# Small products put between large ones on TensorE's turns outside its loop, a narrower wait of VectorE, and a residual product moved at the end

## The reference, cut to what matters

```python
xn = layernorm(x) * ln_w + ln_b
q = softmax(xn @ Wq + bq, over the 32 of a head)
k = softmax(xn @ Wk + bk + (1 - mask) * -1e6, over the 64 tokens)
v = (xn @ Wv + bv) * mask
att = einsum('bnhd,bnhl->bhdl', k, v)
y   = einsum('bnhd,bhdl->bnhl', q, att)
scale, shift = split(silu(emb) @ W_emb + b_emb)
hh  = silu((layernorm(y) * ln2_w + ln2_b) * (1 + scale) + shift) @ W_out + b_out
out = x + hh
```

## Time and profile before

| | us |
|---|---|
| median of 3 runs | 306.57 |
| lowest and highest of them | 304.46 and 307.16 |
| the profiled execution | 304.73 |
| its span, first instruction to last | 302.9 |
| PE busy in the span | 291.5 (96%) |
| DVE busy | 267.8 (88%) |
| POOL busy | 244.5 (81%) |
| ACT busy | 237.2 (78%) |
| granted clock of PE, mean | 0.999 |

### The profile page before, as it was taken

How to read it: one execution, slowest core, us unless ns; L and a number is a source line. 1 busy time by engine, 2 the same in 40 slices (tenths; PEclk the granted TensorE clock), 3 DMA queues, 4 the chain that set the end, 5 groups by cost and what they waited for, 6 DMA issues and landing times.

```text
span 302.9 us, 14378 instructions
## 1 busy us (share of the span) xinstructions
PE 291.5 (96%) x5530; PEld 248.2 (82%) x5530; DVE 267.8 (88%) x637; ACT 237.2 (78%) x592; POOL 244.5 (81%) x248
## 2 busy tenths in 40 slices
PE   7999899999999999999999999999999999999985
PEld 6578787989889898889888898989888898877764
DVE  4898999989999999999999999999999796977773
ACT  1555779697989889888989798888989798786543
POOL 2376489898998989998999989898999979873560
PEclk9999999999999999999999999999999999999999
DMA  6962560806335170907245270806151331002024
GB/s 207 307 244 67 162 188 5 245 4 186 134 115 200 43 269 1 303 9 227 85 133 179 74 239 1 312 1 249 63 183 60 101 142 50 21 4 72 4 71 138
DMA packets 28445, 38.61 MB, mean 127 GB/s; under 512 B 2433, under 2 KB 20481, under 8 KB 28418
## 3 DMA queue, kind: packets, MB, share of 16 engines
q1 hardware_dynamic: 28000, 37.94, 38.1%
q10 hardware_dynamic: 418, 0.30, 0.4%
HBM read 29.80 MB, written 8.45 MB: 126 GB/s over the span
## 4 chain that ended last, share of the span: by engine, by line
PE 86%; DVE 4%; POOL 4%; issue 2%; DMA 1%; ACT 1%; SPq 0%; DVEq 0%; POOLq 0%
PE bk L1156 29%; PE bv L1156 28%; PE by L1156 15%; PE by L1241 4%; PE by L1218 4%; PE bv L1230 4%; DMA x_all<-in_x 1%; DVE xstat L818 1%; POOL x_all L479 1%; POOL xr L459 1%; ACT k_t L661 1%; POOL k_t L428 1%; POOL xr L488 1%; DVE w_qv_lo L893 0%; PE by L1382 0%
## 5 line engine op out<-in xcount | busy, mean ns | idle before, releaser
L661 ACT ACTIVATE k_t<-k_t,kmax 128x64 f32<-128x64 f32 x240 | 60.5, 337 | 5.8 <-DVE kmax L952 5.6
L479 POOL TENSOR_TENSOR x_all<-x_all,bo_all 128x1024 f32 (+1 forms) x16 | 40.1, 2508 | 0.2
L448 POOL TENSOR_TENSOR xt_raw<-xt_raw,rows 128x512 f32<-128x512 f32 x28 | 36.3, 1298 | 4.2 <-DMA rows<-rows_dram 4.2
L450 POOL TENSOR_TENSOR xt_raw<-xt_raw,rows 128x512 f32<-128x512 f32 x28 | 36.1, 1290 | 2.2
L439 POOL TENSOR_TENSOR h_lo<-h_s,h_hi 128x512 fp32r<-128x512 f32 x28 | 35.4, 1287 | 0.5 <-ACT h_hi L680 0.4
L289 POOL TENSOR_TENSOR z_s<-z_s,mod_shift 128x512 f32<-128x512 f32 x30 | 30.7, 1046 | 5.4 <-DVE z_s L966 5.2
L615 ACT ACTIVATE y_s<-y_s,yr 128x256 f32<-128x256 f32 x56 | 29.1, 592 | 5.3 <-POOL yr L471 5.3
L1156 PE MATMUL bv<-w_o_hi,h_hi 128*128 128x256 f32 x112 | 29.4, 284 | 0.0
L1156 PE MATMUL bv<-w_o_lo,h_hi 128*128 128x256 f32 x112 | 28.9, 280 | 0.0
L600 ACT ACTIVATE v_s<-bk,small 128x256 f32<-128x256 f32 x32 | 15.2, 475 | 17.3 <-PE bk L1156 16.0
L1156 PEld LDWEIGHTS by<-kv,q_t 32*64 32x64 f32 x2048 | 22.4, 130 | 7.8 <-issue 5.8
(11 more groups left out here) (171 smaller groups left out, 863.7 us busy)
## 6 DMA issues: line engine op xcount, KB each, us to landing
x_all<-in_x SPq DMA_DIRECT2D x15, 512.0 KB, 6.4
out<-x_all SPq DMA_DIRECT2D x15, 512.0 KB, 5.1
xt_raw<-in_x_t SPq DMA_DIRECT2D x14, 512.0 KB, 5.9
rows<-rows_dram SPq DMA_DIRECT2D x14, 512.0 KB, 4.2
off<-in_mask_rows SPq DMA_DIRECT2D x16, 256.0 KB, 6.0
rows_dram<-xr_rows SPq DMA_DIRECT2D x56, 1.0 KB
x_all<-in_x SPq DMA_DIRECT2D x2, 256.0 KB, 3.7
z_s<-in_w_emb SPq DMA_DIRECT2D x1, 512.0 KB, 7.0
```

What stands on the lines that cost most here:

```text
L448: nc.gpsimd.tensor_tensor(xc, xc, rows[:, parity, 0, :], ALU.mult).then_inc(xm_d, 1)
L450: nc.gpsimd.tensor_tensor(xc, xc, rows[:, parity, 1, :], ALU.add).then_inc(xs_d, 1)
L479: nc.gpsimd.tensor_tensor(xg, xg, bo_all[:, :].unsqueeze(1).broadcast_to([P, T, D]), ALU.add).then_inc(xb_d, 1)
L661: last = nc.scalar.activation(kk, kk, ACT.Exp, scale=-1.0, bias=kmax[:, c, n:n + 1])
```

## The change

- `x_variances` waits for `xmv_d` (the `bn_aggr` of the group before) in place of `xr_d`; the wait for `xr_d` stands ahead of `x_means` now.
- `qv_tile`, `attention` and `y_product` are cut into parts: `qv_part(i, t, n)` is two matmuls of a tile, `attention_tile` and `y_tile` are the products of one tile (16 in the code, 32 pairs in the trace). In turns 2 and 15 PE issues them in turn: attention tile 0, then three times two q/v matmuls of tile 0 and an attention tile, then q/v tile 1; later y tiles 0 and 1, two q/v matmuls of tile 2, y tiles 2 and 3, and the rest of q/v tile 2. The loop's turns and turn 1 keep the order of before.
- In the tail, `x_added(M, 0, bv_)` and the wait for `res_d` ahead of it stand before `half_y_transposed(0)` instead of behind the two tile products.
- `late_out(e)` makes all products with the high part of both tiles, waits for the low part, and makes those with the low part.

```diff
@@ x_variances, x_means (DVE)
-                wait(dve, xr_d, 4 * g)
+                wait(dve, xmv_d, 4 * g)
...
             def x_means(g):
 
+                wait(dve, xr_d, 4 * g)
                 for t in range(T):
@@ qv_tile (PE)
+                for n in range(3):
+                    qv_part(i, t, n)
+
+            def qv_part(i, t, n):
+
+                if n > 0:
+                    pass
+                elif t < 2:
                     wait(pe, qsub_d, 4 * i + t - 3)
                     wait(pe, zs_d, 2 * (i - 2) + t + 1)
                 else:
                     wait(pe, kadd_d, 2 * i + t - 1)
                 tok = slice(t * P, t * P + P)
...
+                a = xt_lo if n == 2 else xt_hi
+                w = w_qv_lo if n == 1 else w_qv_hi
+                for c in range(C):
+                    last = mm(bqv[t][:, :], a[:, c, tok], w[:, c, :], n + c == 0, n == 2 and c == C - 1)
+                if n == 2:
+                    last.then_inc(qv_d, 1)
@@ body (PE)
+                apart = isinstance(i, int) and i >= 2
...
+                if B and apart:
+                    attention_tile(i - 1, 1 - par, 0)
+                    for n in range(3):
+                        qv_part(i, 0, n)
+                        attention_tile(i - 1, 1 - par, n + 1)
+                else:
+                    if B:
+                        attention(i - 1, 1 - par)
                     qv_tile(i, 0)
-                    qv_tile(i, 1)
+                qv_tile(i, 1)
                 if B:
                     wait(pe, h_d, 2 * i - 2)
-                    y_product(i - 1)
-                if F:
+                if B and apart:
+                    y_tile(i - 1, 0)
+                    y_tile(i - 1, 1)
+                    qv_part(i, 2, 0)
+                    y_tile(i - 1, 2)
+                    y_tile(i - 1, 3)
+                    qv_part(i, 2, 1)
+                    qv_part(i, 2, 2)
+                else:
+                    if B:
+                        y_product(i - 1)
                     qv_tile(i, 2)
-                    qv_tile(i, 3)
+                qv_tile(i, 3)
@@ late_out (PE)
-                if e == 0:
-                    pe.wait_ge(hhi_d, 2 * M + 2)
-                out_tiles(bv_[e], h_hi_m, h_lo_m, e,
-                          (lambda: pe.wait_ge(hlo_d, 2 * M + 2)) if e == 0 else None, False).then_inc(o_d, 1)
+                pe.wait_ge(hhi_d, 2 * M + 2)
+                for t in (2 * e, 2 * e + 1):
+                    dst = bv_[e][:, (t % 2) * D:(t % 2) * D + D]
+                    for c in range(C):
+                        mm(dst, h_hi_m[:, c, t * P:t * P + P], w_o_hi[:, c, :], False, False)
+                        mm(dst, h_hi_m[:, c, t * P:t * P + P], w_o_lo[:, c, :], False, False)
+                pe.wait_ge(hlo_d, 2 * M + 2)
+                for t in (2 * e, 2 * e + 1):
...
+                last.then_inc(o_d, 1)
@@ tail (PE)
                 x_added(L, 0, bk_)
+                pe.wait_ge(res_d, 2 * (L - 2) + 2)
+                x_added(M, 0, bv_)
                 half_y_transposed(0)
                 pe.wait_ge(zs_d, 2 * M + 2)
                 x_added_tile(2, bk_[1])
                 x_added_tile(3, bt[0])
-                pe.wait_ge(res_d, 2 * (L - 2) + 2)
-                x_added(M, 0, bv_)
                 x_added(M, 1, bv_)
```

More of the change, by code:

```diff
@@ L1195, in qv_tile @@
             def qv_tile(i, t):
-                if t < 2:
+                for n in range(3):
[4 more added lines that the diff above has]
+                elif t < 2:
                     wait(pe, qsub_d, 4 * i + t - 3)
@@ L1245, in attention @@
             def attention(g, parity):
-                wait(pe, ek_d, 2 * g + 2)
-                wait_apart(pe, v_d, 4 * g + 4)
                 for t in range(T):
-                    for c in range(C):
-                        col = (t * C + c) * AW
-                        for h in range(HC):
[L1252 to L1271, removed]
+                    attention_tile(g, parity, t)
@@ new lines, in attention_tile @@
+            def attention_tile(g, parity, t):
+                if t == 0:
+                    wait(pe, ek_d, 2 * g + 2)
+                    wait_apart(pe, v_d, 4 * g + 4)
+                for c in range(C):
+                    col = (t * C + c) * AW
+                    for h in range(HC):
+                        ch = c * P + h * DH
+                        for e in range(2):
+                            rows = slice(e * SEQ, e * SEQ + SEQ)
+                            last = mm(be[e][h * DH:h * DH + DH, col:col + AW], e_k[rows, t, ch:ch + DH],
+                                      v_s[rows, parity, t, c * HC + h, :], True, True)
+                if t == T - 1:
+                    last.then_inc(att_d, 1)
@@ new lines, in y_product, with y_tile @@
+            def y_product(g):
+                for t in range(T):
+                    y_tile(g, t)
+            def y_tile(g, t):
+                if t == 0:
+                    wait(pe, kv_d, 2 * g + 2)
+                    wait(pe, qt_d, 2 * g + 2)
+                for c in range(C):
+                    col = (t * C + c) * AW
+                    for e in range(2):
+                        b = 2 * t + e
+                        for h in range(HC):
+                            rows = slice(h * DH, h * DH + DH)
+                            last = mm(by[e * SEQ:e * SEQ + SEQ, h, col:col + AW],
+                                      q_t[rows, c, b * SEQ:b * SEQ + SEQ], kv[rows, b, c, :], True, True)
+                if t == T - 1:
+                    last.then_inc(y_d, 1)
@@ L1299, in late_out @@
             def late_out(e):
-                if e == 0:
-                    pe.wait_ge(hhi_d, 2 * M + 2)
-                out_tiles(bv_[e], h_hi_m, h_lo_m, e,
-                          (lambda: pe.wait_ge(hlo_d, 2 * M + 2)) if e == 0 else None, False).then_inc(o_d, 1)
+                pe.wait_ge(hhi_d, 2 * M + 2)
+                for t in (2 * e, 2 * e + 1):
+                    dst = bv_[e][:, (t % 2) * D:(t % 2) * D + D]
+                    for c in range(C):
+                        mm(dst, h_hi_m[:, c, t * P:t * P + P], w_o_hi[:, c, :], False, False)
+                        mm(dst, h_hi_m[:, c, t * P:t * P + P], w_o_lo[:, c, :], False, False)
+                pe.wait_ge(hlo_d, 2 * M + 2)
+                for t in (2 * e, 2 * e + 1):
+                    dst = bv_[e][:, (t % 2) * D:(t % 2) * D + D]
+                    for c in range(C):
+                        last = mm(dst, h_lo_m[:, c, t * P:t * P + P], w_o_hi[:, c, :], False,
+                                  t == 2 * e + 1 and c == C - 1)
+                last.then_inc(o_d, 1)
             def x_transposed(g):
@@ L1352, in body @@
                     q_transposed(i - 1, 1 - par)
-                    attention(i - 1, 1 - par)
-                if F:
-                    if isinstance(i, int) and i == 0:
-                        pe.wait_ge(weights_ready, 2)
+                if first(i):
+                    pe.wait_ge(weights_ready, 2)
+                if B and apart:
[6 more added lines that the diff above has]
+                        attention(i - 1, 1 - par)
                     qv_tile(i, 0)
-                    qv_tile(i, 1)
+                qv_tile(i, 1)
                 if B:
                     wait(pe, h_d, 2 * i - 2)
-                    y_product(i - 1)
-                if F:
+                if B and apart:
[9 more added lines that the diff above has]
+                        y_product(i - 1)
                     qv_tile(i, 2)
-                    qv_tile(i, 3)
+                qv_tile(i, 3)
                 if second(i):
```

## The result

| | before | after |
|---|---|---|
| median of 22 runs each, same chip, us | 305.03 | 306.69 |
| the profiled execution, us | 304.73 | 306.54 |
| its span, us | 302.9 | 304.8 |

The ratio after to before is 1.0044 (95% interval 1.0027 to 1.006): slower by 1.3 us, clear of zero and still within 1%. The forecast was 1.05 us faster. Its 305.5 us lies near 306.69 only by luck: the three runs of before that it was built on had a median 1.5 us above that of the 22. The sign is wrong, and the gain and the loss have to be told apart.

What follows compares the result with a forecast made beforehand. PE, busy 96% of the span, was taken as the bound. Terms: turn 2 +0.5, turn 15 -0.2, statistics' wait -0.9, end -0.45, together -1.05 us, from 306.57 to 305.5 us; range 303.4 to 307.3.

Steps and rivals of the forecast that it cites:

- Interleaving, attention: Turns 2 and 15: attention with q/v tile 0 takes about 2.65 us (bounds 2.2 and 3.1), so `att_d` comes later.
- Interleaving, y: Turns 2 and 15: `y_d` 1.6 us after y's start; turn 2 costs 0.5 us, turn 15 gives 0.2 back.
- speed from the store: Small products on PE: the first ones after large products run faster, taken as 0.5 us off attention with q/v tile 0.
- The wait: Before y of turns 2 and 15: PE idles 0.7 to 0.9 us for DVE's h products, 2.4 us behind `att_d`.
- PE would be even: Turn 2: q/v tile 3 ends at 55.7 us, 55.81 before, if the hole is covered, so PE loses nothing.
- the cases: Whole kernel: the forecast and its three rivals, from 303.6 us (holes all gained) to 307.3 us (late att_d).
- the late att_d costs more than the rest gains: Rival, turns 2 and 15: they cost over 1.35 us together; +0.75 us, 307.3 us; chance 0.15.
- The order does nothing: Rival, turns 2 and 15: instruction blocks come later as PE does, holes reappear further on; -0.15 us, 306.4 us; chance 0.25.
- The h products don't hold y back: Rival, turns 2 and 15: DVE's chain catches up, all three holes are gained; -3.0 us, 303.6 us; chance 0.15.
- Statistics' wait: Turn 0, DVE: its 1.12 us wait for POOL's scale goes, y of turn 1 starts earlier; 0.9 us gained (bounds 0 and 1.1).
- no new bound: Rows' transfer for turn 2: it starts 1.1 us earlier from DVE and limits nothing.
- The end: Tail: `x_added(M, 0)` fills PE's idle 1.46 us, second half transposes start at 292.13 for 292.60; gain 0.45 us (0 to 0.86).

Runs made afterwards that it cites:

- s10: s2 with 4 in place of 9 warming products at the start, ten load-and-matmul pairs fewer: 305.68 us, ratio 0.9998 to the kernel before.
- s2: The changed kernel with TensorE's order as before, leaving the statistics' wait and the end's edits: 303.69 us, ratio 0.9951 to the kernel before.
- s11: s2 with, in turn 15 only, two q/v matmuls put ahead of attention's last tile: 302.63 us, ratio 0.9899 to the kernel before.
- s3: The kernel before with only the changed statistics' wait: 303.97 us, ratio 0.9955.
- s4: The kernel before with only the end's edits, `late_out` and the moved `x_added(M, 0, bv_)`: 305.40 us, ratio 1.0004.
- s1: The kernel before with only the new order of TensorE in turns 2 and 15, attention and y: 308.87 us, ratio 1.0117.
- s5: The kernel before with only attention interleaved with q/v tile 0 in turns 2 and 15, y in one piece: 308.02 us, ratio 1.0084.

## Why the prediction was wrong, point by point

**The step that failed is the size of the interleaved products: 2.65 us for attention with q/v tile 0 in "Interleaving, attention", and 1.6 us from y's start to `y_d` in "Interleaving, y".** They measured 3.28, above the upper bound of 3.1, and 2.52 in turn 2. The weight-load windows of the first tile after:

```profile
45.70:45.80 0.10, 0.10 (x31) 1.00 0.00 0
45.80:45.90 0.10, 0.10 (x27) 1.00 0.00 0
45.90:46.00 0.10, 0.01 (x2) 1.00 0.00 0
```

The last load of a tile does begin within 0.2 us, so the "speed from the store" that I read from the earlier trace rows is there. It shortened nothing: the large matmul behind it starts 0.28 us after the tile did. A round of tile and q/v part takes 0.29 + 0.66 = 0.95 us, where my sum had 0.15 + 0.47 + 0.2 = 0.82, and the part is paid in full by whoever waits for the last tile. (A load of attention lasts 105 ns; the 130 ns of the prediction are those of y.)

The rule of the Trainium skill that the prediction named there ("TensorE: Matmul & The Clock Gate", Part 3, "What overlaps and what doesn't"), that a load overlaps a running matmul only if the row groups differ, points the same way as these rounds, in which each change is paid. The trace doesn't show the rule itself, since the ends of matmuls are modelled.

**The wait was right, the lateness too small.** I had y 0.9 late in turn 2; it started 1.55 later behind attention's start than before (5.76 for 4.21), with the predicted 2.4 us from `att_d` to y holding exactly (49.02 to 51.43). That part of the mechanism, with PE idle 0.7 to 0.9 us before y (0.98 both times), was right. Then "Interleaving, y" had 1.6 us up to `y_d` and it was 2.52: again 0.66 for a q/v part, and 1.00 for the second pair of tiles, which gain no speed. The 0.2 us that stood for this pair doesn't follow from the prediction's own sizes: 0.71 for a pair, less 0.16 for one tile from the store, is 0.55. So `y_d` came 2.6 us late and not 1.1.

From there on two paths lead to y's transposes of turn 3, and they arrive together. PE has work of its own until 63.14, and ACT's normalized y is ready at 63.13:

```profile
61.05 2.08 ACT L615 ACTIVATE y_s<-y_s,yr 128x256 f32<-128x256 f32 x4 [1.98 <-POOL yr L471]
```

The transposes begin at 63.27. So the way over DVE, POOL and ACT, which the prediction took for the price of turn 2, cost at most 0.13 us more than PE's own longer products, and "PE would be even" was wrong. Turn 2 cost 2.04 in place of 0.5 (bounds 0.2 to 1.4), turn 15 cost 0.84 in place of -0.2 (upper bound 0.7). These two make up 2.6 of the 2.9 us between the forecast of -1.05 and the +1.8 of the span. The chances leaned on a misreading too: the cases, 303.6 to 307.3, lie 3.7 us apart, which is more than the 2.7 that the three runs of before spread.

**The rival "the late att_d costs more than the rest gains" is the one that held**, with more than its condition: the turns together cost 2.9, over its 1.35. "The order does nothing" fell for this kernel, whose holes did not come back further on; in s10 one did. "The h products don't hold y back" fell with 0.98 us of idle time.

**"Statistics' wait"**: -0.9 was forecast, and attention of turn 2 is 0.83 earlier in the trace. That they agree is luck: 0.43 of it was there at attention of turn 1 (27.13 for 27.56), whose start varies as much among the runs without the edit (27.09 to 27.61). Alone the edit is worth 1.4 in the median. What I called "no new bound", the rows' transfer, is one. The chain after, turns 1 and 2:

```profile
28.88 4.72 DMA rows<-rows_dram
...
41.63 1.97 ACT y_s L615 x4
43.65 1.09 PE bv L1238 x8
```

From y of turn 1 to attention of turn 2 it took 13.78 us before, 14.33 after, 14.56 and 14.35 in s2 and s11, but 13.57 in s3 and 13.65 in s10. In the longer ones y's transposes wait 0.6 us for ACT's y behind this transfer; in s3 and s10 they don't. Attention of turn 1 to that of turn 2 took 18.94 us before and 17.78 to 18.78 with the edit, so it gains 0.2 to 1.2 us by what the transfer does.

**"The end"**: -0.45 was forecast for the half transposes, and they moved by 0.46. This step was right in place, size and releaser; the path to PE's end took 0.26 less in the whole change and 0.4 less in s4.

## What to carry to other kernels

A product that another engine's long queue waits for is not to be held back to fill gaps behind it: all that is put ahead of its last piece is paid by that queue, here `att_d` came 2.06 us later for 1.4 us of inserted work, and y 1.55. Put filler only at the hole and as little as covers it, as s11 does, and look for the holes again afterwards: ten pairs fewer at the start moved one into turn 4, where it cost 1.4 us. When bounding a mixed order, don't take the speed of one kind of product from a stretch where only that kind runs: read the time from the start of one kind to the start of the next.

## What was not expected of the hardware

**A short stand-still can cost twice.** The granted clock fell to 0.50 not only behind the 2.33 us of idle time of s1, but behind 0.91 us in s2, in the middle of small products and half-idle stretches. A window and the chain of s2:

```profile
54.00:55.00 1.00, 1.00 (x4) 0.74 (x3) 0.97 (x2) 0.00 (x0) 0.92 (x2) 0.50 0.74 199
```

```profile
52.52 0.91 issue
53.42 4.38 PE bk L1157 x11
```

Eleven q/v matmuls took 4.38 us for 2.82, so the hole cost 0.9 and then 1.6. Not each such hole does it: s3 had one of 0.91 and s4 one of 1.11 at the same place and kept their clock. This is much of the scatter between runs of one kernel: beside s1 to s4, 24 of the 29 runs of before had a mean granted clock of 0.997 or more and a median of 305.09, the other 5 one of 308.26.

**The hole behind the same instruction varies.** Behind the first q/v matmul of tile 2 in turn 2 it was 0.35 us before, 0.91 in s2 and s3, 1.11 in s4, 0.23 in s5, 0.60 in s11, with the same products ahead of it, in s5 in another order; the place is fixed by the program, the length is not. It ends 2.3 to 2.7 us behind the burst in each of these traces, and the burst itself shifts against the products. In s4 (window and chain; its y begins at 51.07, that of before at 50.71 with the burst at 50.7):

```profile
51.60:51.70 0.10, 0.10 (x31) 0.10 (x25) 0.10 (x2) 0.10 (x1) 0.10 (x1) 1.00 0.55 164
```

```profile
52.99 1.11 issue
```

The page after has the blocks as a queue of their own:

```profile
q8 instruction: 17, 0.28, 0.4%
```

17 packets of together 0.28 MB are 16 KB each, the size of the bursts in the earlier trace rows.
